# Where the value products and the far transposes stand among five score fills of an attention kernel

## The reference

```python
att = jnp.einsum('bhqd,bhkd->bhqk', q, k) * (1.0 / math.sqrt(hd))
att = jnp.where(causal, att, -jnp.inf)
att = jax.nn.softmax(att, axis=-1)
att = att * decay_weight_matrix(T)      # zero from 512 tokens of distance on
y = jnp.einsum('bhqk,bhkd->bhqd', att, v)
```

## Time and profile before

| | |
|---|---|
| median of 3 runs | 1641.54 us (1638.27 to 1642.66) |
| the profiled execution's own time | 1643.48 us |
| its span in the profile | 1641.7 us |
| ACT busy | 1310.6 us (80%) |
| PE busy | 1295.4 us (79%) |
| DVE busy | 971.1 us (59%) |
| first and last exponential of the attention | 209.75 and 1544.01 us |

### The profile page before, as it was taken

How to read it: one execution, slowest core, us unless ns; L and a number is a source line. 1 busy time by engine, 2 the same in 40 slices (tenths; PEclk the granted TensorE clock), 3 DMA queues, 4 the chain that set the end, 5 groups by cost and what they waited for, 6 DMA issues and landing times. The chain is left out here.

```text
span 1641.7 us, 27956 instructions
## 1 busy us (share of the span) xinstructions
PE 1295.4 (79%) x11067; PEld 756.9 (46%) x11067; DVE 971.1 (59%) x1562; ACT 1310.6 (80%) x2677; POOL 52.4 (3%) x28
## 2 busy tenths in 40 slices
PE   7874178888888888887878888888888888778598
PEld 5532044444444444444444444444444444344287
DVE  4731156666666666666666666666666655554366
ACT  2433089899999999999998989899999999998632
POOL 0211000000000000000000000000000000000022
PEclk9987589999999999999999999999999999997889
DMA  4999940101010101010101010101010101000054
GB/s 149 196 214 200 153 69 1 33 2 33 1 34 1 33 1 33 1 33 1 33 1 33 1 33 1 32 3 24 7 21 10 26 5 30 1 7 0 19 164 134
DMA packets 111721, 72.95 MB, mean 44 GB/s; under 512 B 56395, under 2 KB 110946, under 8 KB 111586
## 3 DMA queue, kind: packets, MB, share of 16 engines
q1 hardware_dynamic: 111586, 71.13, 20.8%
HBM read 45.93 MB, written 25.17 MB: 43 GB/s over the span
## 5 line engine op out<-in xcount | busy, mean ns | idle before, releaser
L777 PE MATMUL fast_s_ps<-k_stack,fast_q_stack 96*128 96x512 bf16 (+3 forms) x2448 | 657.8, 359 | 185.2 <-ACT fast_probs L867 111.3
L867 ACT ACTIVATE fast_s_ps<-fast_s_ps,fast_negmax 128x1024 f32<-128x1024 f32 (+4 forms) x768 | 798.3, 1047 | 5.0 <-PE fast_s_ps L777 4.6
L867 ACT ACTIVATE fast_probs<-fast_s_ps,fast_negmax 128x640 f32<-128x640 f32 (+7 forms) x512 | 442.6, 865 | 122.1 <-DVE fast_negmax L889 121.3
L889 DVE TENSOR_REDUCE fast_negmax<-fast_s_ps 128x1 f32<-128x640 f32 (+4 forms) x512 | 400.5, 782 | 174.0 <-PE fast_s_ps L780 164.0
L897 DVE TENSOR_TENSOR fast_probsT<-fast_t_ps,fast_dec_c 128x640 f32<-128x640 f32 (+4 forms) x512 | 398.9, 779 | 175.3 <-PE fast_t_ps L797 172.6
L777 PEld LDWEIGHTS fast_s_ps<-k_stack,fast_q_stack 96*128 96x128 bf16 x2448 | 175.8, 98 | 462.6 <-ACT fast_probs L867 207.5
L797 PE MATMUL fast_t_ps<-ident,fast_probs 128*128 128x128 f32 x2400 | 360.6, 279 | 23.3 <-DVE fast_y_sb L918 15.6
L797 PEld LDWEIGHTS fast_t_ps<-ident,fast_probs 128*128 128x128 f32 x2400 | 275.6, 142 | 100.9 <-DVE fast_y_sb L918 29.4
L810 PE MATMUL fast_t_ps<-fast_probsT,fast_vals 128*16 128x128 f32 x4800 | 157.1, 275 | 63.9 <-DVE fast_probsT L897 63.4
L867 ACT ACTIVATION_READ_ACCUMULATOR fast_s_ps<-fast_s_ps,fast_negmax 128x1 f32 x768 | 180.3, 235 | 0.0
L810 PEld LDWEIGHTS fast_t_ps<-fast_probsT,fast_vals 128*16 128x16 f32 x4800 | 120.3, 97 | 124.4 <-DVE fast_probsT L897 123.1
(11 more groups left out here) (104 smaller groups left out, 505.1 us busy)
## 6 DMA issues: line engine op xcount, KB each, us to landing
parts_d<-part SPq DMA_DIRECT2D x48, 256.0 KB, 12.8
k_stack<-parts_d SPq DMA_DIRECT2D x48, 256.0 KB, 10.1
fast_q_stack<-parts_d SPq DMA_DIRECT2D x192, 64.0 KB, 3.0
fast_vals<-v_d SPq DMA_DIRECT2D x36, 128.0 KB, 3.2
xs<-x_dram SPq DMA_DIRECT2D x8, 512.0 KB, 8.6
v_d<-w SPq DMA_DIRECT2D x8, 512.0 KB, 8.9
y_d<-fast_y_sb SPq DMA_DIRECT2D x32, 128.0 KB, 2.1
yy<-y_d SPq DMA_DIRECT2D x16, 256.0 KB, 2.7
```

The source lines that it names most:

```text
L777: last = nc.tensor.matmul(s_ps[:, n % SLOTS, o:o + w], q, k_stack[:, h, P * b0 + o:P * b0 + o + w], start=True, stop=not diag)
L867: nc.scalar.activation(dst, src, ACT.Exp, bias=negmax[:, p % 2, side, h:h + 1], scale=-1.0, accum_out=sums[:, p % 2, side, h, c:c + 1]).th ...
L889: nc.vector.tensor_reduce(out=negmax[:, p % 2, side, h:h + 1], in_=s_ps[:, n % SLOTS, max(0, cols - P * WIN):cols], axis=AX_X, op=ALU.min) ...
```

## The change

Each burst moves behind fill 4 and ahead of fill 5, where also the turning back goes. The far burst stays in every fourth step (heads 0, 4, 8, 12), the near one moves to the step two later (heads 2, 6, 10, 14), so that a step has at most one. Turning back and finishing stand in heads 1 and 3 (before: 1 and 2). The far transposes of every step move from ahead of fill 5 to behind it. Since a near burst now runs two steps late, the near part of `probsT` has six slots in place of four (the tile grows from 40 to 50 blocks of 128). `values` is written in two parts, which are called one right behind the other. The DVE instructions follow the same order.

```diff
+            TSLOTS = {FAR: HG, NEAR: HG + 2}
+            TBASE = {FAR: 0, NEAR: HG}
...
+            def turned(side, s):
+                return TBASE[side] + s % TSLOTS[side]
...
+            def group_after(s):
+
+                if s >= HG and s % HG == 0:
+                    return FAR, s // HG - 1
+                if s >= HG and s % HG == 2:
+                    return NEAR, s // HG - 1
+                return None
+
+            def back_after(s):
+
                 p, h = step_of(s)
+                return {1: (FAR, p - 1), 3: (NEAR, p - 1)}.get(h) if p > 0 else None
...
-                probsT = sb("fast_probsT", [P, 2, HG, WIN, P], fp32, s2)
+                probsT = sb("fast_probsT", [P, sum(TSLOTS.values()), WIN, P], fp32, s2)
...
                         fill(s, 1)
-                        if s > 0 and h % HG == 0:
-                            values(FAR, s // HG - 1)
                         fill(s, 2)
-                        if p > 0 and h in (1, 2):
-                            turn_back(p - 1, h - 1)
                         fill(s, 3)
+                        if group_after(s):
+                            values(*group_after(s), 0)
+                            values(*group_after(s), 1)
+                        if back_after(s):
+                            side, done = back_after(s)
+                            turn_back(done, side)
+                        fill(s, 4)
                         turn(FAR, s)
-                        fill(s, 4)
-                        if s > 0 and h % HG == 0:
-                            values(NEAR, s // HG - 1)
...
                         maximum(FAR, s)
                         if s > 0:
                             decay(NEAR, s - 1)
-                        if s > 0 and h % HG == 0:
-                            group_to_sb(FAR, s // HG - 1)
                         maximum(NEAR, s)
-                        if p > 0 and h == 1:
-                            factors(p - 1)
-                        if p > 0 and h in (1, 2):
-                            finish(p - 1, h - 1)
+                        if group_after(s):
+                            group_to_sb(*group_after(s))
+                        if back_after(s):
+                            side, done = back_after(s)
+                            if side == FAR:
+                                factors(done)
+                            finish(done, side)
                         decay(FAR, s)
-                        if s > 0 and h % HG == 0:
-                            group_to_sb(NEAR, s // HG - 1)
```

More of the change, by code:

```diff
@@ L667, in next_turn @@
                 turn_no[job] = len(turn_no)
-            for s in range(NSTEP + 1):
+            def group_after(s):
[5 more added lines that the diff above has]
+            def back_after(s):
                 p, h = step_of(s)
+                return {1: (FAR, p - 1), 3: (NEAR, p - 1)}.get(h) if p > 0 else None
+            for s in range(NSTEP):
                 if s > 0:
                     next_turn("unit", NEAR, s - 1)
-                if s > 0 and h % HG == 0:
[L674 to L679, removed]
-                if p > 0 and h in (1, 2):
-                    next_turn("back", h - 1, p - 1)
-                next_turn("unit", FAR, s)
-                if s > 0 and h % HG == 0:
-                    next_turn("group", NEAR, s // HG - 1)
+                if group_after(s):
+                    next_turn("group", *group_after(s))
+                if back_after(s):
+                    next_turn("back", *back_after(s))
+                next_turn("unit", FAR, s)
+            next_turn("unit", NEAR, NSTEP - 1)
+            for side in (FAR, NEAR):
+                next_turn("group", side, NSTEP // HG - 1)
+            for side in (FAR, NEAR):
+                next_turn("back", side, NPAIR - 1)
             s2 = ExitStack()
@@ L798, in turn, with values @@
                         last.then_inc(turn_full, 1)
-                    def values(side, k):
-                        pe.wait_ge(turn_free, turn_no["group", side, k])
+                    def values(side, k, part):
+                        n = turn_no["group", side, k]
+                        pe.wait_ge(turn_free, n)
                         p, h = step_of(HG * k)
@@ L805, in values @@
                         nb = blocks(i)
-                        if h == 0:
+                        if h == 0 and part == 0:
                             pe.wait_ge(vals_loaded[p % 2], vals_count[p])
-                        for b in range(nb):
+                        half = (nb + 1) // 2
+                        for b in range(half) if part == 0 else range(half, nb):
                             for j in range(HG):
@@ L811, in values @@
                                                         vals[:, side, (i + 1 - nb + b) % VT, HD * (h + j):HD * (h + j + 1)],
-                                                        probsT[:, side, j, b, :], start=(b == 0), stop=(b == nb - 1))
-                        last.then_inc(turn_full, 1)
+                                                        probsT[:, turned(side, HG * k + j), b, :],
+                                                        start=(b == 0), stop=(b == nb - 1))
+                                if b == nb - 1 and j == HG - 1:
+                                    last.then_inc(turn_full, 1)
                     def turn_back(p, side):
@@ L830, in _ @@
                         fill(s, 1)
-                        if s > 0 and h % HG == 0:
-                            values(FAR, s // HG - 1)
                         fill(s, 2)
-                        if p > 0 and h in (1, 2):
-                            turn_back(p - 1, h - 1)
                         fill(s, 3)
+                        if group_after(s):
[5 more added lines that the diff above has]
+                        fill(s, 4)
                         turn(FAR, s)
-                        fill(s, 4)
-                        if s > 0 and h % HG == 0:
-                            values(NEAR, s // HG - 1)
                     pe.wait_ge(exp_done, PER * NSTEP)
                     turn(NEAR, NSTEP - 1)
-                    values(FAR, NSTEP // HG - 1)
-                    values(NEAR, NSTEP // HG - 1)
+                    for side in (FAR, NEAR):
+                        for part in range(2):
+                            values(side, NSTEP // HG - 1, part)
                     turn_back(NPAIR - 1, FAR)
@@ L896, in decay @@
                         nb = blocks(tile_of(p, side))
-                        nc.vector.tensor_tensor(probsT[:, side, h % HG, 0:nb, :],
+                        nc.vector.tensor_tensor(probsT[:, turned(side, s), 0:nb, :],
                                                 t_ps[:, 0:P * nb].rearrange("p (b q) -> p b q", q=P),
@@ L926, in _ @@
                     for s in range(NSTEP):
-                        p, h = step_of(s)
                         maximum(FAR, s)
```

## The result

The changed kernel takes 1660.61 us (median of 4 runs, 1658.39 to 1664.13) against 1640.07 for the kernel before (1638.27 to 1642.66): the ratio is 1.0126, 95% interval 1.01 to 1.0152, 20.5 us slower. The profiled execution took 1658.39 us, its span is 1656.4.

The account below looks back on a forecast made before the run. ACT waiting for DVE's maximum was taken as the bound, with 132.2 us lost. Stalls after the change sum to 143.5, 11 more: 1655 against the profiled 1643.48, given as 1652 us, range 1633 to 1668.

Parts of the forecast that it names:

- quiet steps: Steps without a burst: far decay behind fill 5 delays the far maximum; up to 5.16 us against 4.70, 21 us.
- steps with a burst: Burst behind fill 4, then copy, far transposes, far decay, far maximum: ACT stalls 0.80 in pair 0; 126 steps, 100 us.
- turning back: Factors and finish between near maximum and far decay make a step 0.81 us over 4.70; 15 pairs, 11 us.
- start of the attention: Stall at the attention's start, taken as unchanged from before: 0.5 us.
- falls of the clock: Falls to half clock stretch steps, pairs 5 to 7 and 13 to 15 being thinly used: 11 us, bounds 0 to 20.
- I take 0: At the head of a burst behind fill 4: neither a gap nor a shortening, 0 us each.
- rival 3: Much slower: a gap at the burst's head too, 0.22 x 126 = 28 us more, 1680 us; chance 0.09.
- rival 1: Faster: the burst is shorter behind fill 4, 0.22 us each, 28 less, 1624 us; chance 0.15.
- 132.2 - 123: Before the change: ACT's whole loss in the attention less the bursts' cost, leaving some 9 us for clock falls.
- Rival 4: The DVE order does not bind and all that bursts cost ACT is won: 1518 us; chance 0.02.
- Rival 2: No change: the clock falls no more than before or costs less, 0 to 5 us; 1642 to 1647 us; chance 0.24.

Follow-up runs that it names:

- experiment 5: Changed kernel plus five unused 256-column matmuls in quiet steps of pairs 6, 7, 13, 14 and 15, between fills 4 and 5: 1657.9 us.
- experiment 1: Changed kernel with the far transposes back ahead of fill 5, bursts still behind fill 4: 1655.6 us, 1.0093 of the kernel before.
- experiment 2: Kernel before with only the far transposes moved behind fill 5, two bursts still in every fourth step: 1731.1 us, 1.0556 of the kernel before.
- experiment 6: Changed kernel with one unused 128 by 128 fp32 transpose between fill 4 and each burst: 1678.3 us, a single run.
- experiment 3: Changed kernel with each burst cut to one block, a probe whose value product omits older blocks: 1584.3 us, 0.9662 of the kernel before.
- experiment 7: Changed kernel with the bursts alone moved ahead of fill 4, far transposes still behind fill 5: 1608.0 us, 0.9784 of the kernel before.
- experiment 4: Changed kernel with the bursts moved ahead of fill 4 and the far transposes ahead of fill 5: 1553.2 us, 0.9472 of the kernel before.

## Why the prediction was right in kind and half in size

Slower was right, and the measured 1660.6 lies in the range; 20.5 us were lost where 11 were given. Term by term, the predicted stalls against those read from the starts of exponential 1 in the changed kernel:

| term | predicted | measured |
|---|---|---|
| quiet steps | 21 | 19.4 |
| steps with a burst | 100 | 108.6 |
| turning back | 11 | 10.6 |
| start of the attention | 0.5 | 2.1 |
| falls of the clock | 11 | 12.0 |
| sum | 143.5 | 152.7 |

(A fall is counted as the excess of a long step over steps of its kind in the same pair; in pair 15 over those of experiment 5.)

- *Quiet steps: right.* The chain through fill 5, far transposes, far decay and far maximum was given as 5.16 in pair 7 and is 5.14; pairs 0 to 2 stayed near 4.70. The wait for the maximum came 173 times for 134.9 us, where 200 times and some 120 us were given, and exponential 3 no longer waits, as forecast. Experiment 1 shows that the place causes it, experiment 2 that it does so in the kernel before too.
- *Steps with a burst: the mis-sized term.* The step that failed is "I take 0" for the gap at the burst's head. It is 0.10: fill 4 at 814.32, its four blocks 0.22, the burst at 814.64. The row I leaned on, fill to transposes without a gap, was of the wrong kind; the transition to the burst costs it (experiment 6). The rest of the chain held: copy 1.36 behind the burst's start, far transposes 0.34, far decay 0.80, far maximum 0.75, exponential 0.85, 4.10 as summed. The 0.10, less small errors the other way, is 0.07 a step, 8.6 us in 126. (The prediction's own terms for pairs 8 to 15 add up to 48.9, not 49.5.) So rival 3 was right at half its size, and rival 1 fell: nothing of the burst slips under fill 4. The burst's first weight load starts with the burst, at 814.64. The Trainium skill (TensorE: Matmul & The Clock Gate) says in its architecture section that weight loads can be pulled ahead of running matmuls, and in its Part 3 that this happens only where the row groups differ. The burst fits Part 3, but the far transposes of the same trace do not: their first weight load starts at 821.32, 0.21 ahead of them and while the second matmul of fill 5 runs, though the fill uses 96 rows and they use all 128. So the rows do not explain the burst's gap, and its cause stays open.
- *The clock: the size was right, in part by luck.* Falls came in pair 7 as feared (872.78, a step of 6.09 in place of 5.14, and 7.27 behind it) and in pairs 14 and 15, 12 us in ten steps. In the profile of experiment 5 they cost 6.7. But longer quiet steps as their cause are not shown: experiments 3, 6 and 7 have them in pair 7 without a fall, and experiments 1 and 4 show a fall in pair 1 (7.01) and in pair 8 (6.63) beside quiet steps of 4.71 to 4.74. The 9 us given for falls before the change, 132.2 - 123, came out by luck: the 63 steps with bursts cost 114 and not 123 (their pair-7 row, 6.93 - 4.71, is itself 2.22 and not 1.95), and the 8 us of turning back were left out.
- *What the prediction did not tell:* that 19 of the 20.5 us lie in pairs 12 to 15, where pairs 4 to 7 lose about what the other early pairs win. Its sum held it (49.5 us for bursts in pairs 8 to 15, as for the first half), but the cost of before was taken as 1.95 for all 63 pairs of bursts from one pair's rows, where it runs from 2.3 in pair 0 to about 1 in pair 13 and 0.55 in pair 15.
- *Rival 4,* that the DVE order does not bind, fell with the timeline: each far maximum starts 0.74 to 0.75 behind the far decay, and exponential 1 0.85 behind that; experiment 2 shows the same on the kernel before.
- *Rival 2* fell too, by a little: the falls cost 12 us against about 9 before, not less; without that difference some 17 us would still be lost.

## What to carry to other kernels

When a job is moved into an engine's idle time, look for the idle time that lies ahead of a wait with slack, and follow what comes behind the job on every engine: here, with the far transposes ahead of fill 5, the same burst cost 0.8 to 1.2 us behind fill 4 (experiment 1) and 0.03 to 0.3 ahead of it (experiment 4), because behind fill 4 its copy held the far transposes and, through VectorE's order, the next maximum. Two moves in one change can hide each other: alone, one cost 92 us and the other 16.5, together they cost 20.5, and undoing the first within the change gave back only 5. So try each part alone, from both ends. And a price read from one tile shape should be read again at the others before it is multiplied.

## What the hardware showed unexpectedly

- Going from 128-wide weights to a burst of 16-column weights cost TensorE 0.10 us, behind bf16 fills (814.54 to 814.64) and behind an fp32 transpose (0.20 from start to start, 0.11 of it columns) alike; from the end of the burst's weight loads to the next fill 0.21 to 0.22 passed (815.64 to 815.86). The weights of 128-wide transposes were loaded during the fill ahead of them (821.32), those of the burst were not (814.64).
- The granted clock fell to half (1.2 GHz) in pair 7 although pairs 0 to 6 had run at 1.00, after quiet steps had grown by a tenth. Five extra matmuls of 256 columns in the quiet steps of pairs 13 to 15 went with a clock of 0.96 there in place of 0.93. In pair 7 three kernels stayed at 1.00 without them, so what set off that fall is not shown.
